# A scan and expert kernel: softplus and sigmoid spread over units, a reduction for a cast, and half of the zeroing moved

## The reference

```
xn    = layernorm(x)
dbl   = xn @ x_proj_w.T                       # 128 for delta, 16 for B, 16 for C
delta = softplus(dbl[:128] @ dt_proj_w.T + b)
h[t]  = exp(delta[t] * A) * h[t-1] + delta[t] * B[t] * xn[t]     # 16 states a channel
s     = sum_n(h * C) + xn * D
top2  = top_k(xn @ gate_w + gate_b, 2)        # of 8 experts
f     = mean over top2 of relu(xn @ expert_w[e] + expert_b[e])
out   = x + s * silu(f)
```

## Time and profile before

| | |
|---|---|
| median of 3 runs | 2381.47 us (2371.7 to 2382.94) |
| the profiled execution | 2374.54 us |
| its span in the profile | 2372.8 us |
| TensorE busy | 80% |
| VectorE busy | 85% |
| ScalarE busy | 59% |
| GpSimd busy | 78% |
| mean granted TensorE clock | 0.908 |

### The profile page before, as it was taken

One profiled execution on the slowest core, in us unless ns is written; L12 is line 12 of the kernel. 1 busy time (PEld: TensorE's weight loads), 2 busy tenths in 40 slices (PEclk: granted clock), 3 DMA queues, 4 the chain that ended last, 5 costly groups with the idle time before them and its releaser, 6 DMA issues.

```text
span 2372.8 us, 34130 instructions
## 1 busy us (share of the span) xinstructions
PE 1891.9 (80%) x8688; PEld 1219.2 (51%) x8688; DVE 2014.5 (85%) x2986; ACT 1389.9 (59%) x2370; POOL 1851.5 (78%) x890
## 2 busy tenths in 40 slices
PE   2298887979788797987879888698887979878784
PEld 2165555546455464645546555465554646555452
DVE  4488898989889898898978889898898988889885
ACT  2355756656566565756656566565756656566563
POOL 1468888788887877878778887778888788887894
PEclk8698998989989898998989989798998989989897
DMA  5659688787977879687787987779787787977884
GB/s 222 225 195 361 211 287 288 258 329 221 353 237 245 309 252 353 208 292 277 254 310 235 327 274 242 298 245 353 222 293 269 259 319 234 328 260 247 317 274 129
DMA packets 281695, 641.19 MB, mean 270 GB/s; under 512 B 22528, under 2 KB 23040, under 8 KB 273296
## 3 DMA queue, kind: packets, MB, share of 16 engines
q1 hardware_dynamic: 187792, 445.84, 53.0%
q10 hardware_dynamic: 69120, 125.86, 15.2%
q0 software_dynamic: 24576, 67.13, 10.1%
HBM read 516.58 MB, written 122.16 MB: 269 GB/s over the span
## 4 chain that ended last, share of the span: by engine, by line
DVE 31%; PE 25%; issue 21%; ACT 9%; POOL 9%; DMA 2%; ACTq 1%; DVEq 1%; SPq 1%; POOLq 0%
PE z_ps L1006 16%; DVE scan_ps L859 10%; DVE h_sb L859 5%; POOL dbx L439 5%; DVE p_sb L869 4%; PE y_ps L1023 3%; POOL xs_rows L465 2%; ACT scan_ps L586 2%; DVE topf L787 2%; DVE y_ps L880 1%; PE y_ps L1040 1%; ACT r_sb L607 1%; DVE y_ps L877 1%; PE proj_ps L950 1%; DVE stats L727 1%
## 5 line engine op out<-in xcount | busy, mean ns | idle before, releaser
L439 POOL TENSOR_TENSOR dbx<-b_sb,u_sb 128x2048 f32<-128x2048 f32 x256 | 1188.0, 4641 | 204.5 <-DVE h_sb L859 161.2
L586 ACT ACTIVATE scan_ps<-delta,a_sb 128x512 f32<-128x512 f32 x1024 | 693.7, 688 | 660.6 <-DVE p_sb L869 625.6
L859 DVE TENSOR_TENSOR_SCAN scan_ps<-scan_ps,dbx 128x512 f32<-128x512 f32 x704 | 842.1, 1217 | 228.0 <-ACT scan_ps L586 115.1
L1006 PE MATMUL z_ps<-w_sb,xsT 128*128 128x512 f32 x1920 | 941.7, 636 | 96.7 <-ACT r_sb L607 96.2
L1006 PEld LDWEIGHTS z_ps<-w_sb,xsT 128*128 128x128 f32 x1920 | 372.2, 204 | 508.3 <-issue 507.2
L1023 PE MATMUL y_ps<-ident,p_sb 128*128 128x128 f32 x2816 | 438.0, 290 | 232.2 <-DVE p_sb L869 231.7
L1023 PEld LDWEIGHTS y_ps<-ident,p_sb 128*128 128x128 f32 x2816 | 345.0, 148 | 398.0 <-DVE p_sb L869 290.9
L453 POOL TENSOR_TENSOR pp_sb<-h_sb,c_sb 128x512 f32<-128x512 f32 (+1 forms) x256 | 406.2, 1587 | 179.9 <-PE y_ps L1040 172.7
L869 DVE TENSOR_TENSOR p_sb<-scan_ps,c_sb 128x512 f32<-128x512 f32 x704 | 472.0, 671 | 0.0
L859 DVE TENSOR_TENSOR_SCAN h_sb<-scan_ps,dbx 128x512 f32<-128x512 f32 x320 | 387.3, 1210 | 9.8 <-ACT scan_ps L586 9.7
L1008 PE MATMUL z_ps<-eb_sb,expert_hot 128*128 128x512 f32 x240 | 190.9, 795 | 0.0
(11 more groups left out here) (98 smaller groups left out, 1436.2 us busy)
## 6 DMA issues: line engine op xcount, KB each, us to landing
w_sb<-in_ew SPq DMA_DIRECT2D x240, 1024.0 KB
b_sb<-bc_rows SPq DMA_DIRECT2D x64, 1024.0 KB, 13.6
xs<-xs_rows ACTq DMA_DIRECT2D x240, 256.0 KB
ys_rows<-r_sb ACTq DMA_DIRECT2D x240, 256.0 KB
c_sb<-bc_rows SPq DMA_DIRECT2D x64, 768.0 KB, 15.0
xn<-in_x SPq DMA_DIRECT2D x16, 1024.0 KB, 16.9
c_sb<-bc_rows SPq DMA_DIRECT2D x64, 256.0 KB, 15.0
xo<-in_x SPq DMA_DIRECT2D x64, 256.0 KB
```

The lines of the kernel that those rows point to most:

```text
L439: nc.gpsimd.tensor_tensor(dbx[:, j % 2], b_sb[:, q * QUAD:(q + 1) * QUAD, :], u_sb[:, dt % 2, :].unsqueeze(1).to_broadcast([P, QUAD, T]), ...
L586: nc.scalar.activation(scan_ps[:, j % DA_BANKS, :], delta[:, dt % 2, :], ACT.Exp, scale=a_sb[:, dt, n:n + 1]).then_inc(da_ready, 1)
L859: nc.vector.tensor_tensor_scan(state, bank, dbx[:, q % 2, r, :], 0.0, ALU.mult, ALU.add).then_inc(scanned, 1)
L1006: nc.tensor.matmul(z_ps[:], xsT[:, slot, c, :], w_sb[:, i % WRING, c, :], start=(c == 0), stop=False)
```

## The change

- The four instructions of `softplus` are spread over three units: Abs and Relu in the first, Exp in the next, Ln in the one after, each ahead of that unit's `da_unit`. The three of `sigmoid` go one to a unit.
- `SIG_AT` and `OUT_AT` change; the second output tile's combine moves from unit 31 to unit 32, the unit of the gate, and stands behind it there.
- The tensor_copy of topf is a tensor_reduce over an axis of length one.
- `tiles_to` lies in PSUM; a second tensor_reduce gives `tiles_own` in SBUF, for the subtraction.
- The zeroing has a semaphore for each buffer. The first scatter waits for the first buffer alone, and the second buffer's zeroing is issued behind the first weights and x(1).

```diff
-SIG_AT = (29, 31, 45, 47)
-OUT_AT = (28, 31, 44, 47)
+SIG_AT = (28, 32, 44, 48)
+OUT_AT = (29, 32, 45, 48)
...
-                                 acc[:, 0:n, :]).then_inc(zero_st, 16)
+                                 acc[:, 0:n, :]).then_inc(zero_st[i], 16)
...
+            load_w(0, 0)
+            load_x(1)
+            load_w(0, 1)
             zero_rows(1)
-
-            load_w(0, 0)
-            load_w(0, 1)
-            load_x(1)
...
-                    pool.wait_ge(zero_st, 2 * 4 * 16)
+                    pool.wait_ge(zero_st[par], 4 * 16)
...
+                if is_first(b):
+                    pool.wait_ge(zero_st[1], 4 * 16)
                 for tt in tts:
                     pool.wait_ge(out_st[tt], b * 16)
...
-            def softplus(b, dt, no):
+            def softplus(b, dt, no, part):
...
+                if part == 0:
+                    act.wait_ge(proj_done, no + 1)
+                    act.wait_ge(dbx_ready, from_start((k - 1) * NQ))
+                    nc.scalar.activation(exp_part, proj_ps[:], ACT.Abs, bias=bias).then_inc(sp_step, 1)
+                    nc.scalar.activation(proj_ps[:], proj_ps[:], ACT.Relu, bias=bias).then_inc(sp_max, 1)
+                if part == 1:
+                    act.wait_ge(sp_step, k * 2 + 1)
+                    nc.scalar.activation(exp_part, exp_part, ACT.Exp, scale=-1.0).then_inc(sp_step, 1)
+                if part == 2:
+                    act.wait_ge(sp_step, k * 2 + 2)
+                    nc.scalar.activation(exp_part, exp_part, ACT.Ln, bias=1.0).then_inc(sp_ready, 1)
...
+                    for part in range(3):
+                        name = STEPS.get(j - COPY_LAG - part)
+                        if name == "NZ0" and nxt:
+                            softplus(b + 1, 0, step_no(b, name), part)
+                        elif name and name[0] == "Z":
+                            softplus(b, int(name[1]), step_no(b, name), part)
...
-                    if j in SIG_AT and not is_first(b):
-                        sigmoid(b - 1, SIG_AT.index(j), b * DT + SIG_AT.index(j) // 2 + 1)
+                    for part in range(3):
+                        if j - part in SIG_AT and not is_first(b):
+                            tt = SIG_AT.index(j - part)
+                            sigmoid(b - 1, tt, b * DT + tt // 2 + 1, part)
...
-                nc.vector.tensor_copy(topf[:], topi[:, :, 0:2]).then_inc(gate_step, 1)
+                nc.vector.tensor_reduce(topf[:], topi[:, :, 0:2].unsqueeze(3), AXIS.X, ALU.max).then_inc(gate_step, 1)
...
-                tiles_of = proj_ps[:, 4 * E * BLK:4 * E * BLK + E]
+                tiles_of, tiles_to = proj_ps[:, 4 * E * BLK:4 * E * BLK + E], proj_ps[:, 4 * E * BLK + E:4 * E * BLK + 2 * E]
...
+                nc.vector.tensor_reduce(tiles_own[:], over[:], AXIS.X, ALU.add).then_inc(own_ready, 1)
...
-                nc.vector.tensor_tensor(tiles_from[:], tiles_to[:], tiles_of, ALU.subtract).then_inc(rank_step, 1)
-                nc.vector.tensor_tensor(upto[:], tiles_to[:].unsqueeze(1).to_broadcast([P, TILES, E]),
+                dve.wait_ge(own_ready, b + 1)
+                nc.vector.tensor_tensor(tiles_from[:], tiles_to, tiles_own[:], ALU.subtract).then_inc(rank_step, 1)
+                nc.vector.tensor_tensor(upto[:], tiles_to.unsqueeze(1).to_broadcast([P, TILES, E]),
```

More of the change, by code:

```diff
@@ L141, in build @@
         place = sb("place", [P, E, BLK])
-        tiles_to = sb("tiles_to", [P, E])
+        tiles_own = sb("tiles_own", [P, E])
         over = sb("over", [P, E, E])
@@ L169, in build @@
         out_st = [sem(f"out_st{tt}") for tt in range(TT)]
-        zero_st = sem("zero_st")
+        zero_st = [sem("zero_st0"), sem("zero_st1")]
         sorted_st = sem("sorted_st")
@@ L196, in build @@
         row_sum = sem("row_sum")
+        own_ready = sem("own_ready")
         place_sum = sem("place_sum")
@@ L549, in copy_bc @@
                 nc.scalar.activation(bc_row[:], proj_ps[0:2 * N, :], ACT.Copy).then_inc(proj_used, 1)
-            def softplus(b, dt, no):
+            def softplus(b, dt, no, part):
                 k = b * DT + dt
-                act.wait_ge(proj_done, no + 1)
-                act.wait_ge(dbx_ready, from_start((k - 1) * NQ))
                 bias = db_sb[:, dt:dt + 1]
                 exp_part = u_sb[:, dt % 2, :]
[L558 to L563, removed]
+                if part == 0:
[9 more added lines that the diff above has]
+                    nc.scalar.activation(exp_part, exp_part, ACT.Ln, bias=1.0).then_inc(sp_ready, 1)
             def keep_delta(b, dt):
@@ L623, in store_rows, with sigmoid @@
                 nc.scalar.dma_start(ys_dram[par][i * P:(i + 1) * P, :], r_sb[:, slot]).then_inc(ys_out[slot], 16)
-            def sigmoid(b, tt, copied):
-                act.wait_ge(y_used, copied)
+            def sigmoid(b, tt, copied, part):
                 c = b * TT * 2 + tt * 2
                 z = y_ps[:, tt // 2].rearrange("p t q -> p (t q)")
[L629 to L635, removed]
+                if part == 0:
+                    act.wait_ge(y_used, copied)
+                    act.wait_ge(acc_in[tt], (b + 1) * 32)
+                    act.wait_ge(out_sum, from_start(b * TT + tt))
+                    nc.scalar.activation(z, acc[:, tt], ACT.Exp, scale=-1.0).then_inc(sig_step, 1)
+                if part == 1:
+                    act.wait_ge(sig_step, c + 1)
+                    nc.scalar.activation(z, z, ACT.Ln, bias=1.0).then_inc(sig_step, 1)
+                if part == 2:
+                    act.wait_ge(sig_step, c + 2)
+                    nc.scalar.activation(z, z, ACT.Exp, scale=-1.0).then_inc(sig_ready, 1)
             act.add_instruction(mybir.InstLoadActFuncSet(
@@ L651, in _ @@
             copy_bc(0, step_no(None, "NS"))
-            softplus(0, 0, step_no(None, "NZ0"))
+            for part in range(3):
+                softplus(0, 0, step_no(None, "NZ0"), part)
             keep_delta(0, 0)
@@ L720, in _ @@
             for tt in range(TT):
-                sigmoid(B - 1, tt, B * DT)
+                for part in range(3):
+                    sigmoid(B - 1, tt, B * DT, part)
         @block.vector
@@ L815, in rank @@
                 nc.vector.tensor_reduce(tiles_of, over[:], AXIS.X, ALU.add).then_inc(rank_step, 1)
+                nc.vector.tensor_reduce(tiles_own[:], over[:], AXIS.X, ALU.add).then_inc(own_ready, 1)
                 dve.wait_ge(rank_step, c + 3)
-                nc.vector.tensor_tensor_scan(tiles_to[:], ones[:], tiles_of, 0.0, ALU.mult,
+                nc.vector.tensor_tensor_scan(tiles_to, ones[:], tiles_of, 0.0, ALU.mult,
                                              ALU.add).then_inc(rank_step, 1)
                 dve.wait_ge(rank_step, c + 4)
-                nc.vector.tensor_tensor(tiles_from[:], tiles_to[:], tiles_of, ALU.subtract).then_inc(rank_step, 1)
-                nc.vector.tensor_tensor(upto[:], tiles_to[:].unsqueeze(1).to_broadcast([P, TILES, E]),
+                dve.wait_ge(own_ready, b + 1)
+                nc.vector.tensor_tensor(tiles_from[:], tiles_to, tiles_own[:], ALU.subtract).then_inc(rank_step, 1)
+                nc.vector.tensor_tensor(upto[:], tiles_to.unsqueeze(1).to_broadcast([P, TILES, E]),
                                         iota[:].unsqueeze(2).to_broadcast([P, TILES, E]), ALU.is_le
```

## The result

The median went from 2380.1 us to 2343.2 us (four executions each, interleaved on one chip): ratio 0.985, 95% interval 0.9822 to 0.9878.

A forecast was written before the change was run, and what follows sets the result against it. No engine bounds alone; the chain is split between VectorE and TensorE. Fifteen batches at +0.1 us (+1.5), the start -17 and the last batch's unit 8 -0.9 give -16.4 from 2381.5: 2365 us, range 2318 to 2388.

The forecast's parts named there:

- unit 8: At unit 8 of a batch, Exp and Ln go behind the exponentials of units 8 and 9: -1.2 us.
- Relu and TensorE (units 8 to 28): At unit 15, the first tile's Relu, awaited by TensorE, no longer stands behind Exp and Ln: -0.2 us a batch.
- cast to reduction, and the triple behind the gate: Unit 32: reduction for cast, -0.1 us; tile 1's three VectorE output instructions placed behind the gate, +2.05 us a batch.
- late Ln: At unit 34, the softplus's Ln must wait for unit 35's exponential and comes late: +0.25 us, bounds 0 and 0.6.
- rank: In the ranking, indices come 0.9 to 1.0 us after GpSimd's pp ends rather than 1.65: -0.7 us a batch.
- The start: First scatter waits only for the first half of the zeroing: -17 us once, ends -12 and -18.
- upto and the tensor_scalar behind it: In the ranking, upto stops waiting and takes about 0.3 us; a tensor_scalar and cast behind it may wait for pp.
- The stall moves to hot: Unit 32's gate: the cast's wait passes to hot and covers less; 2354 to 2383 us, chance 0.50.
- the second case: At the gate, VectorE's hot instructions slip in between GpSimd's pp and dbx: -2.75 us a batch, 2322 us, chance 0.28.
- The term +2.05: Unit 32: tile 1's three output instructions, once in the stall's shadow, now come after it: +2.05 us a batch.
- The softplus step: Softplus spread from unit 8: -1.2 us there, -0.2 at unit 15, TensorE otherwise working on with no gap but 0.23 us.
- the likeliest case: At the gate, the stall passes to hot and covers less: 2354 to 2383 us, chance 0.50.

The follow-up runs named there:

- triple31: The changed kernel with the output of tile 1 back in unit 31, ahead of the gate; ratio 0.9661 against the kernel before.
- g30t31: The changed kernel with the gate at unit 30 and the output of tile 1 at unit 31; ratio 0.9656 against the kernel before.

## Why the prediction was right or wrong

By its own steps, a batch, in us:

| step | forecast | measured |
|---|---|---|
| unit 8 | -1.2 | -1.18 |
| Relu and TensorE (units 8 to 28) | -0.2 | -0.19 |
| cast to reduction, and the triple behind the gate | -0.1 + 2.05 | +1.64 |
| late Ln | +0.25 | +0.29 |
| rank | -0.7 | -0.85 |
| units 52 to the next 0 | 0 | -0.76 |
| sum | +0.1 | -1.05 |

- *The start* was forecast at -17. The wait fell by 15.0, since the scatter, held at its "usual 12.7 us", took 15.5; the zeroing alone gave 16.
- *Unit 8, the late Ln, upto and the tensor_scalar behind it* came as written, within 0.15 us each. The second row of the table agrees by luck: the softplus alone gave +0.15 in units 8 to 28, and taken out of the whole change it is worth 1.14 there.
- *The stall moves to hot* was right in 12 batches of 16 (4.50 or 4.51 us). The first had 3.64 us, the second met GpSimd's pause, and in two the second case happened by half: at 276.74 hot slipped in and took 0.28 us, dbx started at 276.93, and hot's twin sat out that dbx for 4.56. The stall ended where it would have. The Trainium skill, "SBUF — State Buffer", "Who interferes with whom", has it that whoever comes first keeps the shared port for the whole instruction; by that, the twin is locked out, and this trace agrees (4.56 us). No row here shows GpSimd waiting for VectorE.
- *The term +2.05* was 0.3 too high; triple31 puts the price of that one placement at 2.03 at the gate and 3.1 a batch with what the clock adds.
- *The step that failed* is the sum itself, "= +0.1 us": it held every TensorE duration fixed and put the stretch from unit 52 to the next 0 at nothing. The softplus step said that TensorE "works on with no gap but 0.23 us" and booked -0.2 for it; it looked at gaps of one place for what they cost directly, and never asked what other gaps do to the clock of the matmuls behind. The profile before had it to read, in rows that I did not look up: a granted clock of 0.908, and the same eight matmuls at 6.73 us in one place and 3.67 in another. What was missed is the wait before unit 60, -0.76 a batch, all of it the shorter duration of tile 13's matmuls; with the gate's 0.3 and rank's 0.15 this is the difference of 1.15 a batch, some 17 us in 15 batches.
- *The prediction's closing list* of what would make it wrong named hot, rank's casts and the zeros. None of them did (the casts did not wait, but the tensor_scalar ahead of them did in their place). The time fell into the stated range because that range reached down to the second case, which did not come; for the likeliest case alone it would have been outside.
- Of the 20.5 us between forecast and medians, 13.2 lie between the forecast and the two profiled spans. The other 7.3 are scatter of executions: before's profiled run lay 5.6 us under its median, after's 1.8 above. Part of such scatter is seen at the very start. The first topf, ahead of which the compute engines do the same in all kernels, starts between 43.8 and 44.7 us in 8 of the 17 profiles (before: 44.33) and between 49.4 and 49.8 in the other 9 (after: 49.59), with nearly every part of the change on either side. Ahead of it lie groups of eight matmuls of 128x168. In before they take 1.41 us from 31.71 on, and its clock rises at 30.0; in after all four take 2.6, as long as before's first did. These 5 us are TensorE's clock and not the change.

What stays open: why the clock's lower stretches fall where they do within a batch. The runs show that filling a pause keeps the clock up there, and that the same pause of 1.95 us is followed by half the clock in one batch and by all of it in another; no run shows which earlier pauses decide it. Open, too, are the 3.4 us by which the stretch from unit 60 to the next batch is longer in every second batch from 3 to 11, in all kernels alike.

## What to carry to other kernels

Before summing an edit, look up whether a group of equal matmuls has two durations at different places, and the granted clock beside each; if it has, an edit that moves pauses ahead of such a group can change its duration by as much as the two differ (3.67 to 6.73 us here), and the sum needs a term with these bounds for the engine that waits behind it. The length of the nearest pause does not give the value. Parts of a change can then not be measured alone and added up. Where a stall on a shared port can't be avoided, put work that doesn't meet it under it, and ahead of the instruction that will wait, not behind: here three instructions with one input in PSUM, at most 0.70 us each, also beside a running dbx.

## What the runs showed of the hardware that was not expected

- Sixteen useless transposes in a pause of TensorE made three kernels faster, by 10 us (after), 13 (before) and 23 to 26 (g30t31, by medians and by ratios); in the first and the last the eight matmuls behind them went from 5.23 or 5.29 us to 3.67.
- The same eight matmuls behind the same pause of 1.95 us took 3.67 us in 10 of 12 batches of triple31 and in 1 of 12 of after, and 5.2 to 5.4 us in the others of after.
- A clock that is kept up at one place may fall for longer at another (0.72 to 0.55 at unit 34, in after with the pause filled).
- A two-input VectorE instruction of 0.2 us that starts 0.06 us after a GpSimd one waits for all of its 4.5 us (12 batches); one that starts 0.19 us ahead of it takes 0.28 us, and GpSimd's starts 1.24 us after its pp, as ever (2 batches). For that one instruction a quarter of a microsecond decides over 4.5 us; the stall as a whole did not get shorter, as its twin then waited.
